# Gathering 424 steps instead of 432 in the five edge stages of a graph network kernel

## The reference

```python
# L0: x @ m, m a product of 50,000 plane rotations (i, j, theta) = (src, dst, edge_weight)
# L1: gate, then three relational attentions (heads 4, 4, 1; widths 512, 512, 128):
alpha = leaky_relu(xw[etype, dst] @ Q + xw[etype, src] @ K, 0.2)
alpha = segment_softmax(alpha, dst, n)
msg = (xw[etype, src].reshape(-1, heads, out_ch) * alpha[..., None]).reshape(-1, heads * out_ch)
h = segment_sum(msg, dst, num_segments=n) + b
# L2: filter; ssp(x) = softplus(x) - log 2
Wf = ssp(ssp(edge_attr @ m1_W + m1_b) @ m2_W + m2_b) * C[:, None]
agg = segment_sum(h1[src] * Wf, dst, num_segments=n_nodes)
# L3: mean over the edges that leave a node
agg = segment_sum(h[dst], src, num_segments=n); out = agg / degree(src)
```

## Time and profile before

| | |
|---|---|
| median of 3 runs | 6628.7 us (6625.01 to 6634.23) |
| the profiled execution | 6613.5 us, span of its instructions 6611.7 us |
| busy: PE, PEld, DVE, ACT, POOL | 66%, 47%, 48%, 30%, 54% of the span |
| mean granted TensorE clock | 0.76 |
| DMA | 565.41 MB, mean 86 GB/s |

### The profile page before, as it was taken

How to read it: one execution, slowest core, us unless ns; L and a number is a source line. 1 busy time by engine, 2 the same in 40 slices (tenths; PEclk the granted TensorE clock), 3 DMA queues, 4 the chain that set the end, 5 groups by cost and what they waited for, 6 DMA issues and landing times. The chain is left out here.

```text
span 6611.7 us, 81270 instructions
## 1 busy us (share of the span) xinstructions
PE 4356.9 (66%) x17924; PEld 3140.3 (47%) x17925; DVE 3158.4 (48%) x7294; ACT 2007.4 (30%) x4713; POOL 3596.5 (54%) x2941
## 2 busy tenths in 40 slices
PE   5599720785776779676677544448788888765553
PEld 5588610443554555355556533334455555443332
DVE  6577556122554532354453244443466666433334
ACT  0122200001655520265552022211566666410000
POOL 0244410366776637776674788760355555238884
PEclk6799955797887879788786555555899999876565
DMA  0000011324665523566551233332333333233333
GB/s 7 24 10 11 10 31 42 91 62 107 168 163 138 150 72 74 127 167 157 137 151 42 46 85 84 85 77 75 80 93 94 94 94 93 67 86 84 84 84 73
DMA packets 515758, 565.41 MB, mean 86 GB/s; under 512 B 308626, under 2 KB 400639, under 8 KB 515225
## 3 DMA queue, kind: packets, MB, share of 16 engines
q0 software_dynamic: 359872, 381.65, 23.9%
q1 hardware_dynamic: 155606, 181.09, 9.7%
HBM read 467.37 MB, written 92.22 MB: 85 GB/s over the span
## 5 line engine op out<-in xcount | busy, mean ns | idle before, releaser
L1200 POOL DMA_INDIRECT sum_gx_sb<-scratch_xw,keep_k_row_step_sb x1296 | 1609.4, 1242 | 560.0 <-issue 361.5
L1313 PE MATMUL sum_a_ps<-sum_gx_sb,sum_sel_sb 125*125 125x258 f32 (+1 forms) x4320 | 1232.0, 450 | 554.3 <-ACT sum_gx_sb L1249 250.5
L1313 PEld LDWEIGHTS sum_a_ps<-sum_gx_sb,sum_sel_sb 125*125 125x125 f32 x4320 | 950.7, 246 | 750.6 <-issue 556.5
L1249 ACT ACTIVATE sum_gx_sb<-sum_gx_sb,sum_wt_sb 125x129 f32<-125x129 f32 x3312 | 981.7, 388 | 468.6 <-DVE sum_wt_sb L1441 468.6
L2377 POOL DMA_INDIRECT filter_gx_sb<-scratch_h,keep_k_src_step_sb x432 | 519.5, 1202 | 540.9 <-DVEq L2522 394.3
L2809 POOL DMA_INDIRECT source_gx_sb<-scratch_h,source_grouped_sb x432 | 533.6, 1235 | 155.9 <-issue 117.6
L2821 PE MATMUL source_s_ps<-source_gx_sb,source_sel_sb 125*125 125x257 f32 x864 | 376.9, 613 | 312.0 <-DMA source_gx_sb<-scratch_h,source_grouped_sb 312.0
L1107 POOL DMA_INDIRECT scratch_grouped<-keep_k_value_sb,keep_k_place_sb x400 | 476.2, 1191 | 123.7 <-issue 123.7
L2821 PEld LDWEIGHTS source_s_ps<-source_gx_sb,source_sel_sb 125*125 125x125 f32 x864 | 251.5, 305 | 437.2 <-issue 173.7
L2431 PE MATMUL filter_ps<-filter_m_sb,filter_h_sb 128*125 128x256 f32 x1760 | 407.1, 385 | 50.7 <-DVE filter_f_sb L2496 50.7
L2431 PEld LDWEIGHTS filter_ps<-filter_m_sb,filter_h_sb 128*125 128x125 f32 x1760 | 322.4, 188 | 180.5 <-issue 135.6
(11 more groups left out here) (503 smaller groups left out, 7102.6 us busy)
## 6 DMA issues: line engine op xcount, KB each, us to landing
scratch_hots<-sum_cuts_sb SPq DMA_DIRECT2D x108, 244.1 KB
filter_sel_sb<-scratch_hots SPq DMA_DIRECT2D x108, 244.1 KB
sum_gx_sb<-scratch_xw,keep_k_row_step_sb POOLq DMA_INDIRECT x1296
scratch_xw<-gate_xsb_sb SPq DMA_DIRECT2D x50, 253.9 KB
scratch_xw<-attend_xsb_sb SPq DMA_DIRECT2D x50, 253.9 KB
filter_ea_sb<-in_ea_t SPq DMA_DIRECT2D x444, 24.4 KB
filter_gx_sb<-scratch_h,keep_k_src_step_sb POOLq DMA_INDIRECT x432
source_gx_sb<-scratch_h,source_grouped_sb POOLq DMA_INDIRECT x432
```

Source lines behind the costliest of these rows:

```text
L1200: nc.gpsimd.indirect_dma_start(out=gx[:, q, j, :], out_offset=None, in_=table, in_offset=bass.IndirectOffsetOnAxis(ap=keep["row_step"][:, ...
L1249: last = nc.scalar.activation(here, here, ACT.Copy, scale=wt[q][:, h, j:j + 1])
L1313: last = mm(psa[b][0:P, half, 0:BF], sel[:, 0, p, j, :], gx[:, q, at, half * BF:(half + 1) * BF], **flags)
```

## The change

GpSimd issues 424 gathers in each of the five phases. In `attention` all else keeps 432 steps; the last 8 columns of the last block of `gx` keep what an earlier block left there, and the wait of the last score is lower by 8 DMAs. `filter` has 53 turns. `source` has 106 halves: 26 turns and two halves written out on TensorE, 25 turns and six halves written out on VectorE. The lists, and their making, keep 432 columns.

```diff
-KS = -(-(ET + NT - 1) // U) * U
+STEPS = ET + NT - 1
+KS = -(-STEPS // U) * U
@@ attention, gpsimd
-            for step in range(KS):
+            for step in range(STEPS):
@@ attention, vector
             def score(s, q, landings):
-                dve.wait_ge(x_in[q], landings * (16 * T))
+                missing = KS - STEPS if isinstance(s, int) and s == NS - 1 else 0
+                dve.wait_ge(x_in[q], landings * (16 * T) - 16 * missing)
@@ filter_sum
-    TURNS, U2 = KS // (2 * HF), 2 * HF
+    TURNS, U2 = STEPS // (2 * HF), 2 * HF
-            for step in range(KS):
+            for step in range(STEPS):
@@ source_mean
-    HALVES = KS // HF
+    HALVES = STEPS // HF
+    TURNS, LEFT = divmod(HALVES, RING)
-            for step in range(KS):
+            for step in range(STEPS):
@@ source_mean, tensor
-            with pe.Fori(0, HALVES // RING) as i:
+            with pe.Fori(0, TURNS) as i:
                 for q in range(RING):
                     sums(i * RING + q, i, q)
+            for q in range(LEFT):
+                sums(TURNS * RING + q, TURNS, q)
@@ source_mean, vector
-            with dve.Fori(0, HALVES // RING - 1) as i:
+            with dve.Fori(0, TURNS - 1) as i:
                 for q in range(RING):
                     add(i * RING + q, q)
                     pick(i * RING + q + 2, q)
-            for q in range(RING):
-                add(HALVES - RING + q, q)
-                if q + 2 < RING:
-                    pick(HALVES - RING + q + 2, q)
+            for h in range((TURNS - 1) * RING, HALVES):
+                add(h, h % RING)
+                if h + 2 < HALVES:
+                    pick(h + 2, h % RING)
```

## The result

Median of six runs each: 6586.03 us (6580.65 to 6589.27) against 6626.08 us before (6621.01 to 6634.23), 40.05 us less. The ratio is 0.9938, with a 95% interval of 0.9925 to 0.9951 (32 to 50 us faster). The prediction was 6589.2, 39.5 us less. A second series of the same kernel on another chip gave 6597.47 against 6636.74, 39.3 us less, ratio 0.9936 (0.9923 to 0.9949).

What follows compares the result with a forecast made beforehand. No engine was busy over two thirds of the span; each stage, ending in a barrier, had its own bound. Savings of 0 + 0 + 7.8 + 18.5 + 13.2 = 39.5 us from the 6628.7 median gave 6589.2 us, range 6575 to 6602.

Steps and rivals of the forecast that it cites:

- sum1 and sum2, 0: Ends of sum1 and sum2: the last gather is in time, VectorE and TensorE set the end; 0 gained, at most 0.35 us.
- sum3, 7.8: End of sum3: the last score's 8.05 us wait for its gather goes, less some 0.2 us of issue; 7.8 us gained.
- Filter, 18.5: Filter: VectorE sets the pace, and 53 turns instead of 54 save one turn of 18.54 us; bounds 18.1 and 19.0.
- Source, 13.2: Source: 12.06 us from issuing eight fewer gathers plus 1.15 from a shorter last lag; 13.2 us, bounds 12.0 and 15.0.
- The lag: End of source: time from the last half's last gather to its first add falls from 8.45 to 7.3 us, gaining 1.15.
- the prediction's second argument: End of source: half 107, with nothing queued behind it, was 1.3 us quicker than 106, pointing to a lag of 7.2.
- Leaving the loop, 0: Straight code behind TensorE's source loop: leaving the loop costs 0, at the most 1.94 us.
- The clock: Filtered stage: a mean granted clock moved from 0.77 was named as a sign that the forecast is wrong.
- The slower case: Filtered stage falls to the lower clock throughout, kernel 41 us slower at 6670; decided at mean clock 0.61; chance 0.02.
- Gathers everywhere: Rival: gathers bind in all stages, 12.06 us each in sum1 and sum2 too; 63.6 us in all, 6565.1; chance 0.03.
- Only the filter: Rival: sum3 and source gain nothing, 18.5 us alone, 6610.2; chance 0.07, including the filter and one more.
- Does less: Rival: the change removes less than it says, though counts are fixed in code; chance 0.01.

Runs made afterwards that it cites:

- attention as a whole: Changed kernel with filter and source put back, so only the three attention stages issue 424 gathers: 6611.44 us, ratio 0.9985 to the kernel before.
- the filter alone: Kernel before with only the filter cut to 53 turns and 424 gathers: 6603.94 us, ratio 0.9971.
- source alone: Changed kernel with attention and filter put back, so only the source stage has 106 halves: 6606.90 us, ratio 0.9980 to the kernel before.
- the kernel with own rows: Kernel before (432 steps), with lane p of each padding gather in the source list reading row p, not row 0: 6646.07 us in one run, 6629.25 before.
- the last kernel above: Changed kernel with block 35 of each attention stage worked for its 4 used steps only, and own rows in the source list's padding: 6581.43 us, ratio 0.9921 to before.

## Why the prediction was right

*sum1 and sum2, 0.* Shown: the distance to the last score is the same to 0.03 us with 424 and with 432 gathers. A GpSimd that was 72% busy suggested 12 us for each; the score without a wait decided.

*sum3, 7.8.* Measured 7.9 in the distance between the last scores, and 9.3 to 9.9 for attention as a whole by the times. The assumption that everything behind the score moves with it held: from the score to the step that follows the stage it is 35.0 us in all traces of the uncut kernels. In another execution the wait would have been 5.60 us, so this term depends on the trace that it is read from by 2.4 us. Over the whole of sum3, first gather to the step that follows, the four traces with 432 gathers have 707.9 to 714.3 us and the four with 424 and the rest of the stage unshortened 701.5 to 704.3, 7.9 less on average.

*Filter, 18.5.* Measured 18.58 in the trace, 16.8 to 19.2 by the times of the filter alone. The table above has 16.9 because the first two halves took 10.92 and 9.70 us in the changed kernel's trace instead of 9.99 and 9.52, and the first product came 0.6 us later after the first gather. That isn't the change's: source alone, with the filter unchanged, has 10.9 and 9.70 too, and a later kernel with 53 turns has 9.99 and 9.53.

*Source, 13.2.* Measured 13.2 to 13.8 by the times of source alone, with an interval from 7 to 20. The traces are sharper, and say that the term was 2 us too large. The stage up to the mean is 674.4 to 675.0 us with 432 steps and 663.3 to 664.7 with 424, 11 less on average, not 12.06 + 1.15. The part of the issue is what fell short. The last gather was to start 12.06 us earlier after the first one; it started 655.1, 654.2 and 652.9 us after it in the three traces with 424 steps, where the kernel before has 663.6: 8.6 to 10.7 earlier. The gathers up to step 423 took 1.3 to 3.5 us longer than the 651.6 of the trace before, on which the term rests. Between the traces of before and after the pauses are the same (128.9 us in all), and single gathers are longer: what they take above 1.20 us each sums to 17.5 us, against 14.0 before (the first gather left out). It doesn't hang on the shorter loops: the kernel with own rows has 432 steps and the old loops, and its gathers up to step 423 take 654.8 us, with 17.3 above 1.20. So it moves from one execution to the next; what lengthens single gathers stays open.

The lag was the smaller part, and was forecast as 7.3 us; it came to 6.53, 6.37 and 7.32, a gain of 1.1 to 2.1 instead of 1.15. The working behind the 7.3 is half right. A backlog that grows by 0.59 us with each half fits the halves 103 and 104 (6.09 and 6.51 in the kernel before, for 6.1 and 6.7) but not 105, which has 8.48 there. What stands behind a half adds to its lag as well, as the prediction's second argument (half 107 against 106) had it.

The Trainium skill ("DMA: Bandwidth & Descriptors", section "Anatomy of one DMA — SWDGE (gpsimd) path") gives one DMA a fixed cost and one for its bytes, and says nothing of which rows it reads. The traces don't agree with that for the rows here: with equal bytes the last lag is 5.78 us with own rows and 8.45 with one row. By that rule the lag would have stayed at 8.45; it fell by 1.1 to 2.1.

*Leaving the loop, 0.* Shown by the timeline of TensorE in the changed kernel, at the last halves of source; the last two stand in straight code. The idle time ahead of each ends with the landing of its data, none with issue. That ahead of the first behind the loop (3.19 us) is the longest of the three, which is the backlog of padding and not the exit: where the padding has own rows and the same loops (the last kernel above), the idle time ahead of half 104 is 2.37 us and its lag 5.71, against lags of 4.9 to 5.9 inside the loop.

```profile
6514.12 3.50 PE L2824 MATMUL source_s_ps<-source_gx_sb,source_sel_sb 125*125 125x257 f32 x8 [2.60 <-DMA source_gx_sb<-scratch_h,source_grouped_sb]
...
6520.81 3.57 PE L2824 MATMUL source_s_ps<-source_gx_sb,source_sel_sb 125*125 125x257 f32 x8 [3.19 <-DMA source_gx_sb<-scratch_h,source_grouped_sb]
...
6527.27 3.15 PE L2824 MATMUL source_s_ps<-source_gx_sb,source_sel_sb 125*125 125x257 f32 x7 [2.89 <-DMA source_gx_sb<-scratch_h,source_grouped_sb]
```

*The clock.* The mean of the filtered stage did move from 0.77 to 0.75, which I had named as a sign against the forecast. It was a badly chosen sign: the stage took 4.4 us more in this trace, but the traces of the other kernels, which change nothing in it, have means from 0.74 to 0.78. The slower case would have needed 0.61.

*The rivals.* Gathers everywhere wanted 32 us from attention and got under 10. Only the filter: attention and source alone are each faster, with intervals that leave out 1. "Does less": the page counts 424.

That the sum of 39.5 met 40.05 to within 1 us is partly luck. By the traces the terms are 0, 7.9, 18.6 and 11, which makes 37.5; the measured 40 has an interval of 32 to 50, which holds both. And medians of the same kernel differ by 11 us between series (6626 and 6637 before), and the traces of before and after by 27 us.

## What to carry to other kernels

Padding that is cut from the end of a stage is worth what the stage waits for at that end: nothing where the last consumer doesn't wait, the wait itself where it does, and a whole turn where the loop's own pace binds. So read the last wait of each stage, not the busy share of the engine that loses the work. When the change is 0.6% and single executions differ by 0.4%, check it by distances between two instructions near the edit, which agreed to 0.03 us here while the length of a whole stage moved by 10 us. And look at which rows the padding lanes read: of the two choices tried here, one row for all loaded the DMA engines more than a row for each. For some twenty gathers at the end of a stage that was worth some 2 us, and nothing that the times show; for a stage full of them it was 47.

What the padding costs the other engines can be worth more than its transfers: leaving the 8 steps out of the arithmetic of the last attention blocks too saved some 19 us in the three stages (some 4.5 of them came back in the filter), beside the 8 us that leaving out their gathers had saved there.

## What was not expected of the hardware

- Indirect gathers in which all 125 lanes read the same row land slower than others of equal size: 1.645 us for each against 1.549 when all 424 of a stage are such, with the DMA engines busy for 0.98 of the time against 0.37. The lag of a half rises from some 5.7 us to 8 to 10 when some twenty of them end a stage, and to 16 to 20 for most halves (12 to 23 for all but the first two) where all gathers are such and the ring of buffers holds GpSimd back.
- The wait for issue at the head of a loop went from 0.48 to 0.57 us per turn when code of another stage was shortened (975.0 to 979.5 us for the filter). It may be where the loop's instructions then lie; that wasn't tested and stays open.
- The 456 matmuls of the filtered stage took 146.7 to 156.8 us, at mean granted clocks of 0.78 to 0.74, with no difference in the work.
